# Moving VectorE's second weight sum of a step behind the row maxima of its burst

## The reference, cut to what matters

```python
Q = _split_heads(x, H)
K = _split_heads(x @ Wk + bk, H)
V = _split_heads(x @ Wv + bv, H)
mask = jnp.where(causal, 0.0, -jnp.inf).astype(x.dtype)
scores = jnp.einsum('bhqd,bhkd->bhqk', Q, K) + mask
attn = jax.nn.softmax(scores, axis=-1)
o = jnp.einsum('bhqk,bhkd->bhqd', attn, V)
o = o.transpose(0, 2, 1, 3).reshape(B, S, -1)
x = x + gelu(o) @ Wf + bf      # then layer norm, gated feed-forward, layer norm
```

## Time and profile before

| what | value |
|---|---|
| median of 3 runs | 2063.76 us (2058.99 to 2065.08) |
| the profiled execution | 2059.51 us, span 2057.8 us |
| TensorE matmul busy | 1888.7 us (92%) |
| VectorE busy | 1527.1 us (74%) |
| ScalarE busy | 1041.1 us (51%) |
| GpSimd busy | 1127.8 us (55%) |
| mean granted TensorE clock | 0.959 |

### The profile page before, as it was taken

One profiled execution on the slowest core, in us unless ns is written; L12 is line 12 of the kernel. 1 busy time (PEld: TensorE's weight loads), 2 busy tenths in 40 slices (PEclk: granted clock), 3 DMA queues, 4 the chain that ended last, 5 costly groups with the idle time before them and its releaser, 6 DMA issues. The chain is left out here.

```text
span 2057.8 us, 38524 instructions
## 1 busy us (share of the span) xinstructions
PE 1888.7 (92%) x10304; PEld 975.6 (47%) x10304; DVE 1527.1 (74%) x3598; ACT 1041.1 (51%) x1523; POOL 1127.8 (55%) x1192
## 2 busy tenths in 40 slices
PE   6799999999999999999999999688879899999896
PEld 4344444444444444444444443233356666666664
DVE  3887878878788788887888878777156767676764
ACT  2255555555555555555555555444534545454543
POOL 0176776767767777677776776766511212121212
PEclk9799999999999999999999999987889999999998
DMA  9645536445364453654546544732147464747430
GB/s 306 200 135 154 174 111 193 150 142 184 105 190 156 139 180 113 183 152 146 173 123 178 153 144 131 199 93 59 53 114 188 120 188 118 191 118 192 119 105 21
DMA packets 260995, 303.24 MB, mean 147 GB/s; under 512 B 28065, under 2 KB 177697, under 8 KB 260913
## 3 DMA queue, kind: packets, MB, share of 16 engines
q1 hardware_dynamic: 260912, 302.25, 51.0%
HBM read 174.20 MB, written 127.93 MB: 147 GB/s over the span
## 5 line engine op out<-in xcount | busy, mean ns | idle before, releaser
L935 ACT ACTIVATE weights<-ring 128x1024 f32<-128x1024 f32 (+3 forms) x768 | 601.2, 810 | 370.1 <-PE ring L682 352.1
L652 POOL TENSOR_TENSOR weight_sum<-weight_sum,weights 128x512 f32<-128x512 f32 (+3 forms) x448 | 683.4, 1525 | 9.6
L682 PE MATMUL o_acc<-weights,v_pair 128*64 128x512 f32 (+3 forms) x3072 | 623.1, 513 | 6.5 <-POOL weights L630 5.9
L630 POOL TENSOR_SCALAR_AFFINE_SELECT weights<-weights 128x256 f32<-128x256 f32 x512 | 220.2, 435 | 356.5 <-ACT weights L935 350.2
L1085 DVE TENSOR_REDUCE part_max<-ring 128x2 f32<-128x1024 f32 x256 | 300.3, 1215 | 104.2 <-PE ring L682 104.2
L682 PE MATMUL ring<-q_stack,k_stack 50*128 50x512 f32 (+3 forms) x1536 | 315.6, 417 | 61.6 <-DVE rowmax L1093 27.6
L673 POOL TENSOR_TENSOR h_lo<-hidden,h_hi 128x512 f16<-128x512 f32 x96 | 114.1, 1190 | 449.8 <-ACT h_hi L903 449.8
L682 PE MATMUL ring<-k_stack,q_stack 48*128 48x512 f32 (+3 forms) x1536 | 307.7, 404 | 23.2 <-DMA k_stack<-k_rows 13.3
L1093 DVE CUSTOM_DVE_ANT_0 scrap<-ring,causal 128x128 bf16<-128x128 f32 (+3 forms) x512 | 229.3, 485 | 81.7 <-PE ring L682 81.3
L1093 DVE CUSTOM_DVE_ANT_0 scrap<-ring,causal,part_max 128x128 bf16<-128x128 f32 (+3 forms) x512 | 251.2, 547 | 47.7 <-PE ring L682 47.3
L682 PEld LDWEIGHTS o_acc<-weights,v_pair 128*64 128x64 f32 x3072 | 174.6, 138 | 228.6 <-issue 198.9
(11 more groups left out here) (105 smaller groups left out, 2162.6 us busy)
## 6 DMA issues: line engine op xcount, KB each, us to landing
v_pairs<-v_unit SPq DMA_DIRECT2D x64, 512.0 KB, 5.7
v_pair<-v_pairs SPq DMA_DIRECT2D x64, 512.0 KB, 5.5
o_heads<-o_pair SPq DMA_DIRECT2D x64, 512.0 KB, 5.2
g<-o_heads SPq DMA_DIRECT2D x16, 2048.0 KB, 8.2
den_wide<-reciprocals SPq DMA_DIRECT2D x32, 1024.0 KB, 16.7
q_stack<-q_rows SPq DMA_DIRECT2D x128, 192.0 KB, 3.6
k_stack<-k_rows SPq DMA_DIRECT2D x128, 192.0 KB, 4.2
q_rows<-x_hi SPq DMA_DIRECT2D x32, 512.0 KB, 5.1
```

What stands on the lines that cost most here:

```text
L630: pool.affine_select(out=diag, in_=diag, compare_op=ALU.is_ge, fill=0.0, base=0, pattern=[[0, 2], [1, P]], channel_multiplier=-1).then_inc ...
L652: pool.tensor_tensor(dst, other, W[t][:, :, :], ALU.add).then_inc(s_add, 1)
L682: return nc.tensor.matmul(o, l, r, start=start, stop=stop)
L935: nc.scalar.activation(W[t][:, :, :], bank_of("t", t)[:, :, 0:width_of(t)], ACT.Exp).then_inc(s_w, 1)
```

## The change

`carry_sum` of pair n-2 is issued in burst 5 behind the loop over the ring tiles of the burst, that is behind `top(7)` and `top(8)`, instead of ahead of them. In D `reciprocals` follows it. No operation is added or removed, and all waits stay as they are.

```diff
                     if b == 0 and 1 <= r <= PAIRS:
                         shift_hi(r - 1, n - 1)
-                    if b == 5 and LEAD <= r < PAIRS + LEAD:
-                        carry_sum(n - LEAD)
                     for what, j in uses(b):
                         if what == "s" and r < PAIRS:
                             top(j, r, n)
@@
                     if b == 4 and LEAD <= r < PAIRS + LEAD:
                         begin_sum(r - LEAD, n - LEAD)
+                    if b == 5 and LEAD <= r < PAIRS + LEAD:
+                        carry_sum(n - LEAD)
                     if a is not None and k == 0:
                         if b == 2:
                             x_part1(a)
```

## The result

The changed kernel takes 2074.92 us (median of 7 runs, 2069.32 to 2079.29) against 2065.08 us for the kernel before in the same comparison: a ratio of 1.0052, 95% interval 1.0032 to 1.0073. It was forecast to be faster, at 2055.3 us, and the measured time is outside the range of 2040 to 2072. The profiled executions have spans of 2069.6 and 2057.8 us, 11.8 us apart.

The account below looks back on a forecast made before the run. TensorE was taken as the bound, with only its gaps to win. Net gains of 0.4 to 0.65 us a period over 14 periods, taken as 7, plus 1.5 at the stage's end gave 8.5 us: 2055.3 us, range 2040 to 2072.

Parts of the forecast that it names:

- D: Steps with r divisible by 4, last of each period of four; direct gain forecast as given back, net 0.
- The bound and the room: Middle stage: TensorE is the bound; only its waits on row maxima can be won, 2.1 us a period of four steps.
- The direct gain in D: At scoreT(9) in the fourth step of a period, TensorE's wait of 0.63 us was to be won.
- B: Second step of a period: subtraction held by add(10), scoreT(4) late; a loss of 0.25 us, or nothing.
- A: First step of a period: shift CAST and subtraction end sooner, the 0.52 us wait at scoreT(4) goes; gain 0.5 plus 0.04 us.
- mask 8: GpSimd's mask coming up with the moved sum: sum goes first by some 0.03 us, making add(7) 1.1 us later.
- the term of C: Third step of a period: delayed add(1) holds large CAST x_hi about 1 us; TensorE loses about 0.7 us, 0.3 net.
- the small CAST: Shift CAST in the fourth step, 0.23 us before: meets the later add(10), about 1.1 us longer, giving the gain back.
- the end of the stage: Steps from r = 56 without jobs: three steps by 0.5 us were to gain 1.5 us.
- rival 3: Slower: TensorE waits for GpSimd's delayed chain at weigh(11) and the subtraction behind add(10); 2075.7 us; chance 0.15.
- Rival 1: Waits are won and nothing given back: 1.8 us a period, 25 us, 2038.5 us; chance 0.15 with what lies between.

Follow-up runs that it names:

- late_D: The kernel before with carry_sum moved late only in the steps with r divisible by 4; ratio to before 0.9960, mean period 85.48 us.
- early_x3: The kernel before, carry_sum still early, with the large CAST x_hi issued one burst later (burst 3); ratio to before 1.0004, mean period 86.19 us.
- early_delay_x3: The kernel before with an unused GpSimd addition ahead of add 7 and the large CAST x_hi one burst later; ratio to before 0.9990, mean period 86.49 us.
- late_x3: The changed kernel, carry_sum late in all steps, with the large CAST x_hi one burst later; ratio to before 0.9899, mean period 85.19 us.
- late_notB_x3: The changed kernel with carry_sum early again in every second step of four and x_hi one burst later; ratio to before 0.9923, mean period 84.86 us.

## Why the prediction was wrong, point by point

**What held.** The bound and the room (2.1 us a period) were right: the best version got 1.2 of them. The direct gain in D was right, 0.58 us measured alone in late_D against 0.63. The sum indeed delayed GpSimd and the delayed GpSimd met VectorE's CASTs and subtractions elsewhere. B lost 0.36 us (0.25 forecast). A gained 0.4 (0.54 forecast): its wait at scoreT(4) of 0.52 us is gone, with 0.19 us at weigh(11) in its place, where 0.15 was reckoned. Rows of the changed kernel in A:

```profile
950.40 0.41 POOL L630 TENSOR_SCALAR_AFFINE_SELECT weights<-weights 128x256 f32<-128x256 f32 x1 [5.72 <-ACT weights L935]
951.96 2.37 POOL L652 TENSOR_TENSOR weight_sum<-weight_sum,weights 128x1024 f32<-128x1024 f32 x1 [1.16 <-DVE weight_sum L1132]
...
956.16 0.92 DVE L1105 CAST shift_parts<-rowmax 128x16 fp32r<-128x16 f32 x1
...
957.70 1.52 DVE L1109 TENSOR_TENSOR shift_parts<-rowmax,shift_parts 128x16 fp32r<-128x16 f32 x1
...
959.60 0.44 PE L682 MATMUL o_acc<-weights,v_pair 128*64 128x128 f32 x4 [0.19 <-POOL weights L630]
```

**Who went first.** I let the sum win against mask 8 by 0.03 us. The mask won, here by 0.09 us (950.40 against 950.49), and in all but one of the 36 steps A, B and C of the twelve periods: the mask kept its 0.41 us, the sum took 1.39, and add 7 started 1.56 us behind the mask in place of 0.37. That is 1.2 us late, where 1.1 was taken and 1.3 to 1.5 given for this order. Two events that close can't be ordered from a trace of another kernel, but here the price of each order was nearly the same.

**The step that failed** is the term of C, "It ends about 1 us later ... 0.3 us net". The place, the cause and the sign were right, the size was not. I let the CAST be held by the one addition that it meets. It was held by three instructions: 2.4 us longer and not 1, and TensorE waited 1.76 us there and not 0.7. From C to D that is a loss of 1.3 us at full clock where 0.3 was forecast. The hold that was forecast did come in three of the twelve periods, with a CAST of 2.25 to 2.35 us, and there C to D lost nothing (21.6 us). This was to be seen before: in the earlier trace rows add 1 ended at 821.92 and the CAST at 822.82, 0.9 us later, and not the 0.3 us that the prediction took as its whole hold, while the same CAST takes 0.68 us when nothing holds it; so it had waited on past add 1 even then, to the end of mask 3. I had no row of a CAST that was alone. The table of the tile's durations, with its minimum of 0.686 us, would have given one.

**The term that was missing** is the clock. A wait of 1.25 and one of 0.51 us close together cost 1.56 us more in half of the periods. The prediction put no term for it into the stage with jobs; it spoke of the clock only for the last steps.

**Errors the other way.** D was to give its gain back through the small CAST. The small CAST took 0.17 to 0.86 us there, not over 1, and in the periods at full clock D kept its gain (21.7 against 22.4 us). And the end of the stage gained 5.4 us (6.6 less the 1.2 of the sum's place), not 1.5; but from the thirteenth A to the last sum the two kernels with an early sum and no delay, before and early_x3, differ by 5.0 us themselves (272.7 and 277.7), so this size is from one execution each.

**The rivals.** The sign was that of rival 3, not its mechanism. It put the price at weigh(11) and the subtraction in B and D: TensorE's waits for masks are 3.2 us in 1090, B lost 0.36 us a period, and D kept its gain at full clock. early_delay_x3 shows that with GpSimd as late as here these cost nothing on balance in eight of twelve periods. Rival 1, the waits won and nothing given back, is what late_x3 and late_notB_x3 come nearest to, with the CAST moved: 0.9 and 1.2 us of its 1.8 a period.

By the Trainium skill (SBUF — State Buffer, "Who interferes with whom") a cast between tiles in SBUF can run in a mode that takes the port pair shared with GpSimd, and whoever issues first has the pair for its whole instruction while the other waits. The traces agree that the CAST is held while GpSimd's instruction runs. The 3.59 and the 2.35 us show what the rule does not say: the one that waits is not always next, and instructions that follow closely on GpSimd's queue can pass it, as mask 3 did, which started at 918.51, 1.39 us behind the CAST. The measurement decides.

**Open.** Why some such CASTs get in after one or two GpSimd instructions and others after three or five; why the clock dropped behind one wait of 1.25 us and not behind one of 1.23 (at 1010.11 us) or 1.27 (at 487.40 us); and how much the end of the stage gains.

## What to carry to other kernels

When an instruction is moved on one engine, write down whose queue waits for it, and shift that whole queue in time against everything that it can't run beside: here a gain of 0.6 us a period was paid for several bursts later, by a CAST that nobody had moved. Price a possible hold by the run of instructions on the other engine, not by the one that is met. When such a collision is found, moving the victim one burst, into the other engine's idle time, can decide the sign of the change: alone the move was worth nothing here, with the change it turned a loss of 0.5% into a gain of 1%.

## What the runs showed of the hardware that I had not expected

A CAST of 128x1024 from fp32, alone 0.68 us, took up to 3.6 us beside a run of GpSimd instructions, and one of 128x16, alone 0.17 us, up to 2.35. A subtraction with both inputs in SBUF, alone 0.17 us, took up to 1.8. TensorE's clock fell from 2.4 to 1.2 GHz at 924.4 us, 1.4 us behind the end of the second of two waits that together were 1.76 us, and was back at 927.8 us, although TensorE was busy without a break from 923.03 us on.
